# Gated cross attention with a two-expert layer: where statistics, normalisations and gating stand in VectorE's order, and a rebuilt prologue

## The reference

```python
q = (xn @ Wq + bq).reshape(B, T, H, hd)
k = (xfn @ Wk + bk).reshape(B, N, H, hd)
v = (xfn @ Wv + bv).reshape(B, N, H, hd)
w = softmax(einsum('bthd,bnhd->bhtn', q, k) / sqrt(hd))
y = einsum('bhtn,bnhd->bthd', w, v).reshape(B, T, D)
...
logits = xf @ w_router
top_vals, top_idx = top_k(logits, 2)
h = square(relu(einsum('nc,ecd->ned', xf, w1)))
y_all = einsum('ned,edc->nec', h, w2)
out = sum(take_along_axis(y_all, top_idx[:, :, None], axis=1) * softmax(top_vals)[:, :, None], axis=1)
...
x = x + tanh(g_xattn[0]) * xattn(layernorm(x), ctx_768, ...)
x = x + tanh(g_ffn[0]) * ffn(layernorm(x), ...)
```

## Time and profile before

| | |
|---|---|
| time, median of 3 runs | 363.44 us (362.04 to 373.72) |
| the profiled execution | 362.29 us |
| its span | 360.5 us |
| its mean granted TensorE clock | 0.969 |
| instructions | 7799 |

### The profile page before, as it was taken

How to read it: one execution, slowest core, us unless ns; L and a number is a source line. 1 busy time by engine, 2 the same in 40 slices (tenths; PEclk the granted TensorE clock), 3 DMA queues, 4 the chain that set the end, 5 groups by cost and what they waited for, 6 DMA issues and landing times.

```text
span 360.5 us, 7799 instructions
## 1 busy us (share of the span) xinstructions
PE 296.0 (82%) x2823; PEld 242.1 (67%) x2823; DVE 230.1 (64%) x932; ACT 180.8 (50%) x410; POOL 107.7 (30%) x188
## 2 busy tenths in 40 slices
PE   0686988889698979888898979897999899877795
PEld 0444576567576767777677867786788788665684
DVE  5595576567557775777667766778567656534455
ACT  1234454545365546455555646464656455533273
POOL 6381815226113350315131613141132100211000
PEclk9997899999899999999999989999999999989899
DMA  3511401074607453463528270835174520250001
GB/s 81 155 47 31 111 20 49 16 118 90 235 4 111 66 185 126 92 85 108 204 53 125 69 244 24 114 44 194 79 110 60 181 90 3 56 213 0 2 30 30
DMA packets 18918, 32.92 MB, mean 91 GB/s; under 512 B 4921, under 2 KB 12058, under 8 KB 18880
## 3 DMA queue, kind: packets, MB, share of 16 engines
q1 hardware_dynamic: 14814, 24.71, 27.8%
q0 software_dynamic: 3216, 7.66, 8.9%
q10 hardware_dynamic: 850, 0.05, 0.2%
HBM read 21.04 MB, written 2.21 MB: 65 GB/s over the span
## 4 chain that ended last, share of the span: by engine, by line
PE 44%; DVE 24%; DMA 11%; ACT 8%; issue 6%; SPq 2%; DVEq 0%; ACTq 0%
PE y L584 12%; PE c L539 7%; DMA gb<-gates_scratch 5%; DVE u L1082 5%; PE ab L495 5%; ACT hs L796 3%; DMA gates_scratch<-gatesT 3%; DMA qs<-q_lo 2%; PE ab L562 2%; PE ab L437 2%; DVE negm L963 2%; PE ab L445 2%; PE h L470 2%; PE ab L428 2%; SPq L317 1%
## 5 line engine op out<-in xcount | busy, mean ns | idle before, releaser
L963 DVE TENSOR_REDUCE negm<-ab 128x4 f32<-128x308 f32 x128 | 60.3, 474 | 73.3 <-PE ab L495 73.0
L791 ACT ACTIVATE p<-s 77x512 f32<-77x512 f32 x128 | 74.3, 583 | 18.4 <-PE s L516 18.4
L584 PE MATMUL y<-w2s,hs 128*128 128x128 f32 x448 | 66.1, 294 | 17.0 <-ACT hs L796 16.9
L584 PEld LDWEIGHTS y<-w2s,hs 128*128 128x128 f32 x448 | 59.9, 206 | 20.6 <-ACT hs L796 20.3
L516 PEld LDWEIGHTS s<-qs,ks 104*77 104x77 f32 x512 | 53.5, 148 | 12.5 <-issue 4.9
L495 PE MATMUL ab<-ks,qs 96*128 96x312 f32 x128 | 50.5, 397 | 13.6 <-ACT cnT L715 9.6
L516 PE MATMUL s<-qs,ks 104*77 104x128 f32 x512 | 56.8, 234 | 2.7 <-ACT p L791 2.6
L796 ACT ACTIVATE hs<-u 128x512 f32<-128x512 f32 x56 | 35.1, 627 | 34.6 <-DVE u L1082 34.4
L1246 POOL TENSOR_SCALAR rs<-mv 128x1 f32<-128x1 f32 x32 | 7.5, 235 | 122.9 <-DVE mv L1004 122.8
L1082 DVE SCALAR_TENSOR_TENSOR u<-h,gb 128x512 f32<-128x512 f32 x56 | 36.7, 673 | 5.6 <-DMA gb<-gates_scratch 3.7
L495 PEld LDWEIGHTS ab<-ks,qs 96*128 96x128 f32 x128 | 24.8, 194 | 18.9 <-ACT cnT L715 10.7
(11 more groups left out here) (130 smaller groups left out, 512.1 us busy)
## 6 DMA issues: line engine op xcount, KB each, us to landing
gb<-gates_scratch SPq DMA_DIRECT2D x14, 768.0 KB, 6.0
gb<-gates_scratch SPq DMA_DIRECT2D x7, 512.0 KB, 3.7
qs<-q_hi SPq DMA_DIRECT2D x12, 256.0 KB, 5.7
ks<-k_hi SPq DMA_DIRECT2D x60, 39.0 KB
x_res<-in_x_dram POOLq DMA_DIRECT2D x8, 256.0 KB, 8.0
out_dram<-y_out POOLq DMA_DIRECT2D x7, 256.0 KB, 5.5
x_sb<-in_x_dram POOLq DMA_DIRECT2D x6, 256.0 KB, 3.5
qs<-q_lo SPq DMA_DIRECT2D x6, 256.0 KB, 7.6
```

Of the source, the lines that this page charges most:

```text
L584: mm = nc.tensor.matmul(bank_y[:, D * b:D * b + D], hs[:, e % 2, T * b:T * b + T], w2s[:, e, :], start=(e == 0 and b == 0), stop=(e == E - ...
L791: nc.scalar.activation(p32[:, m % LR, :], src, ACT.Exp).then_inc(p_done, 1)
L963: nc.vector.tensor_reduce(negm[:, :, c], bank_ab[bank][:, 0:J * NP].rearrange("t (i n) -> t i n", n=NP)[:, :, 0:N], AX.X, ALU.max, negate= ...
```

## The change

*VectorE, steps 1 to 5:* the statistics of the tile after next stand between the row maxima of slot 0, `normalise_ctx` between those of slot 1, `normalise_x` between those of slot 2 (step 0: statistics in slot 1, normalisation in slot 2). In slots 0 and 1 the residual add and its statistics come after the first gated product; in slot 1 all of `gate` comes ahead of the residual, its last four pieces after the first gated product.

*TensorE and ScalarE:* `transpose_ctx` stands behind `max_turn`, `transpose_x` ahead of the output products of slot 2; `gates_turn` stands ahead of the output products of slot 1, `gate_rows` behind the third exponential. `evacuate_ctxT` stands ahead of slot 2's first square.

*GpSimd:* `norm_rstd` moves from slot 2 to slot 0 (step 0: slot 1), behind `rstd`.

*Prologue:* context of tile 0 first on SP's queue, the input of tile 0 first on ScalarE's; weights counted by four semaphores instead of one; tile 0's keys are projected right after its context transpose; tile 1 is transposed in slot 3 of step -1, its keys and query rows are made in slot 0 of step 0; expert loads go to ScalarE's queue in step -1, `prepare_experts` in four parts to slots 1, 2, 3 of step 0 and 0 of step 1, `low_experts` in two parts; the value tile 0 is cleared by GpSimd, the key tile 1 in eight pieces; fewer `keep_on`. Four uses of the `ab` banks are moved in their order.

```diff
-AB_SHIFT = {name: -shift for shift, name in AB_USES}
...
+AB_MOVED = [(("k", 0), ("ctxT", 0)), (("ctxT", 1), ("mT1", 0)), (("xT", 1), ("s1b2", 0)), (("k", 1), ("s1d2", 0))]
...
+                turned = third if j == (3 if i == -1 else 2) else None
+                made = (1, 1) if (i, j) == (0, 0) else third if j == 3 and i != -1 else None
...
@@ SP
-            load(0, 0)
+            sp.dma_start(ctx_sb[:, 0], ctx_v[0]).then_inc(ctx_first[0], 16)
...
@@ TensorE, step
                     if near[0]:
                         scoresT(*near[0], 2)
                     if j == 1 and nxt:
                         project_values(nxt[0])
-                    if i == -1 and j >= 2:
-                        keep_on(bank_s2[1], 2)
                     if i == 0 or (i == 1 and j < 2):
                         keep_on(bank_h[0], 2)
                     if near[2]:
                         max_turn(*near[2])
-                    if j == 3 and third:
-                        (project_queries if i >= 0 else project_query_rows)(third[0])
+                    if turned:
+                        transpose_ctx(turned[0])
+                    if turned and turned[0] == 0:
+                        project_keys(0)
+                    if made:
+                        (project_queries if made[0] >= 2 else project_query_rows)(made[0])
                     if e[2] is not None:
                         hidden(sf, pf, e[2])
...
-                    if j == 2 and third:
-                        transpose_ctx(third[0])
                     if near[3]:
                         scores(*near[3], 0)
                     if (i, j) == (-1, 3):
-                        keep_on(bank_s2[1], 4)
+                        keep_on(bank_s2[1], 2)
                     if near[1]:
                         scoresT(*near[1], 0)
+                    if j == 1 and spread(i - 1):
+                        gates_turn(i - 1)
                     if e[1] is not None and j != 2:
                         output_of(sf, pf, e[1])
                     if near[3]:
                         scores(*near[3], 1)
-                    if i == 0 or (i == 1 and j < 2):
+                    if (i == 0 and j > 0) or (i == 1 and j < 2):
                         keep_on(bank_h[1], 2 if i else 1)
+                    if turned:
+                        transpose_x(turned[0])
                     if e[1] is not None and j == 2:
                         output_of(sf, pf, e[1])
-                    if j == 2 and third:
-                        transpose_x(third[0])
-                    if j == 1 and spread(i - 1):
-                        gates_turn(i - 1)
@@ ScalarE
+            act.dma_start(x_sb[:, 0], x_v[0]).then_inc(x_first[0], 16)
...
-                    if e[1] is not None:
+                    if turned:
+                        evacuate_ctxT(turned[0])
+                    if turned and turned[0] == 0:
+                        evacuate_k(*turned)
+                    if e[1] is not None and j != 2:
                         squared(sf, e[1])
...
                     if near[0]:
                         exponent(*near[0], 3)
+                    if j == 1 and spread(i - 1):
+                        gate_rows(i - 1)
+                    if e[1] is not None and j == 2:
+                        squared(sf, e[1])
@@ VectorE, step
+                    if third and i >= 0 and j == (1 if i == 0 else 0):
                         prepare = stats(*third)
+                        ahead = prepare
+                    if third and i > 0 and j == 1:
+                        ahead = normalise_ctx(*third)
+                    if third and i > 0 and j == 2:
+                        ahead = normalise_x(*third)
...
                     take(top_scores)
+                    take(ahead)
                     take(top_scores)
+                    take(ahead, 2 if ahead is prepare and j < 2 else 1)
                     take(top_scores)
...
                     if near[-2]:
                         low_x(*near[-2])
-                    take(gating)
-                    take(gating)
-                    take(top_scores)
+                    take(gating, 3)
+                    if j in (2, 3):
+                        take(post)
+                        take(post)
                     if j == 2 and exists(i - 2) and not last(i - 2):
                         finish(i - 2, par)
-                    take(gating)
-                    take(post)
...
+                    if j == 2:
+                        take(post)
+                    if j == 3:
+                        take(prepare)
+                        take(post)
                     if e[1] is not None and not (i >= S and near[-2] and not near[-1]):
                         gated_or_weighed(sf, pf, e[1])
+                    take(gating, 4)
+                    take(post, 3)
+                    take(prepare)
@@ GpSimd, step
                     if (i, j) == (-1, 0):
+                        clear_values(pool, nc.gpsimd, 0)
+                        norm_rstd(1, "ctx")
+                        norm_rstd(1, "x")
+                        for c in range(NC):
+                            for half in range(2):
+                                nc.gpsimd.memset(ks[:, 1, c, 2 * half:2 * half + 2].bitcast(F32),
+                                                 0.0).then_inc(zeroed[1], 1)
...
+                    if (i, j) in ((0, 3), (1, 0)):
+                        low_experts(i)
```

More of the change, by code:

```diff
@@ L41, with ab_sequence @@
 ]
-AB_SHIFT = {name: -shift for shift, name in AB_USES}
-def ab_order(step, tiles):
-    return [name for shift, name in AB_USES
+AB_MOVED = [(("k", 0), ("ctxT", 0)), (("ctxT", 1), ("mT1", 0)), (("xT", 1), ("s1b2", 0)), (("k", 1), ("s1d2", 0))]
+def ab_sequence(tiles):
+    uses = [(name, step + shift) for step in range(-2, tiles + 1) for shift, name in AB_USES
             if 0 <= step + shift < tiles and (name, step + shift) not in (("q", 0), ("q", 1))]
-STATS = ["ctx_stats", "x_stats", "ctx_moments", "x_moments"]
+    for moved, behind in AB_MOVED:
+        uses.remove(moved)
+        uses.insert(uses.index(behind) + 1, moved)
+    return {use: k for k, use in enumerate(uses)}
+STATS = ["ctx_stats", "ctx_moments", "x_stats", "x_moments"]
 NORM = ["ctx_normed", "x_normed"]
@@ L226, in apart @@
             eng.sem_inc(held_apart, 1)
+        ab_turns = ab_sequence(S)
         def ab(s, name):
-            step = s + AB_SHIFT[name]
-            k = sum(len(ab_order(t, S)) for t in range(-2, step)) + ab_order(step, S).index(name)
+            k = ab_turns[name, s]
             return k % 2, k // 2 + 1
@@ L374, in unit_rows @@
                         .then_inc(ones_in[par], 16)
-            unit_rows(0)
             def step(i, par):
-                for j, near, nxt, third, ffn in slots(i, par):
+                for j, near, nxt, third, turned, made, ffn in slots(i, par):
                     if near[2]:
```

208 lines of the change are left out of this document (108 added, 100 removed).

## The result

The changed kernel takes 347.45 us (median of 4 runs, 345.29 to 354.17), the kernel before 366.09 in the same comparison (4 runs, 362.04 to 373.72): a ratio of 0.955, 95% interval 0.945 to 0.965. The profiled execution took 348.87 us against 362.29, so 13.4 of the 29.3 us forecast came. The time lies in the stated range, near its upper end, which stood at 349 for the sake of R1, and outside the likeliest case's own 325 to 342; the size of the change does not agree with the sum behind it.

A forecast was written before the change was run, and what follows sets the result against it. It took the kernel to be bound by TensorE, plus a serial chain per slot from VectorE's order of work, plus a prologue. From 362.3 us, 19.8 for the steps and 9.5 for the prologue gave 333.0; range 324 to 349.

The forecast's parts named there:

- R1: Steady steps: inserted work makes row maxima late, the step stays near 38 us, only the prologue pays; 350 us, chance 0.13.
- the likeliest case: Whole kernel: steady steps and prologue both gain; 333.0 us, own range 325 to 342, chance 0.62.
- Slot 0, 1.2 us: Steady slot 0: statistics between maxima remove the 1.0 us wait for the square, 0.4 of the next 0.6 remains; gain 1.2.
- Slot 2, 2.5 less 0.3: Steady slot 2: context waits of 1.1 and 1.4 us go, gain 2.5, less 0.3 per step for sharing transfers.
- Gating earlier: Slot 1: gating ahead of the residual starts the two transfers behind it some 1.2 us earlier.
- R4: Steady steps: gates come too late for new places on TensorE and ScalarE, prologue costs more; about 358 us, chance 0.08.
- parts 1 and 2: Tile steps: statistics and normalisations between maxima, and gating ahead of the residual; gain 19.8 us, bounds 6 to 25.
- (a): Prologue: split loads and keys projected first bring the first scores 3.0 us earlier, to 19.9; bounds 1 to 4.
- (b): Prologue: first to first transposed scores takes 8 us instead of 19.9, two slots of 3.5 plus filler; gain 8 to 13.
- (c): Slot 0 of step 0: tile 1's keys and query rows moved there cost 4.0 us, plus 1.4 for lower clock.
- R3: Step 0 on: fewer fillers leave TensorE's clock at 0.50 until slot 2 of step 1; 375 us, chance 0.04.
- R2: Prologue: two load queues win nothing, first statistics stay at 6.2 us, prologue gives 4; 338.5 us, chance 0.13.

The follow-up runs named there:

- maximum_first_slot2: Changed kernel with the next batch's first maximum ahead of the second gated product in slot 2; 347.27 us, ratio 0.947 to the kernel before.
- prologue_only: Changed kernel with the old order from step 1 on, keeping the new prologue and step 0; 367.47 us, ratio 1.010 to the kernel before.
- more_fillers: Changed kernel with more filler matmuls in step -1 and ahead of the first transposed scores; 346.57 us, ratio 0.954 to the kernel before.
- all_mended: The last experiment: prologue_mended and maximum_first_slot2 together, plus 3 fillers in slot 1 of step 0; 338.75 us, ratio 0.936 to the kernel before.
- prologue_mended: Changed kernel with no clearing beside the first cast, more fillers in step -1, low query rows ahead of the next maximum; 340.94 us, ratio 0.935.
- slot0_as_before: Changed kernel with VectorE's old order in slot 0 from step 1 on; 359.21 us, ratio 0.990 to the kernel before.

## Why the prediction was right or wrong

**Bottleneck: right.** TensorE's waits behind VectorE's order were what could be won; nearly all of the gain is there (0.958 by itself).

**Slot 0, 1.2 us: measured 0.9** (0.84 to 0.92 in steps 2 to 5). The wait for the square (1.0) went as forecast. The residual's chain, of which I kept 0.4, is late by 0.79. The order is worth more than this difference, though: undone alone, inside the new kernel, slot 0 takes 1.1 to 2.5 us more, and the ratio goes from 0.955 to 0.990, some 12 us. I priced it by its wait, not by the clock that follows: 5.6 us in that run's steps 3 and 4, against 4.4 for the waits of four steps.

**Slot 1, 0: measured -0.35.** The wait for x2 of 0.55 is new: with the gating first, the residual and its normalisation come later in this slot.

**Slot 2, 2.5 less 0.3: measured 1.4 to 2.5, mean 1.9.** Both waits went. Late next was neither the gates nor the square but the bank held by a maximum, 0.85; `maximum_first_slot2` brought 0.6 of it. I had named a maximum that the score matmuls wait for as what would prove me wrong; here the input's transposes wait for one, and it costs a part of the gain.

**Gating earlier, 1.2 us earlier and nothing by itself: too small.** The gates' store went out 6.75 us after the slot's value products (159.27 less 152.52), before it was 8.19 (164.94 less 156.75): 1.4 earlier, as reckoned. But without it the new slot 2 is 2.5 to 3.6 us longer, 1.3 of it the longer wait (2.2 for 0.9), the rest not split; the clock has a part in it (0.91 from 125 to 165 us), and the residual's place may have one. The 356 us are near R4's 358, but not by R4's way: there the gates were too late for their new places on TensorE and ScalarE, here for their use on VectorE, with the places as before. The change as made avoids it. I had no term for what it protects.

**Steps 1, 6 and 7: right.** Slot 2 of step 1 gave 3.7 for 3.0, steps 6 and 7 gave 2.0 for 2.0, and slots 0 and 1 of step 1 nothing, with the forecast wait for tile 2's stack:

```profile
PE ab L503 <- DMA qs<-q_lo: 1.3, 1, 1.3
```

The steady step is 35.6 us, not 34.6, and parts 1 and 2 gave 16.5 of 19.8 us (9.8 + 2.0 + 3.7 + 1.0). This alone would have been a fair forecast.

**The prologue, 9.5 us: this is the step that failed.** It gave minus 3.7 with the slots up to slot 2 of step 1 (without slot 2 of step 0, which is in parts 1 and 2), and nothing when tried alone (1.010). The lower bound of 4 did not follow from its own terms either: 1 + 8 - 8 - 1.4 is -0.4. By its terms:

(a) 3.0 earlier: measured 1.9, within its bounds.

(b) 8 us from first to first transposed scores, 11.9 less than before: measured 12.6, so 7.4 less, under its lower bound of 8. The two slots took 5.3 and 4.05 us where the sum has 3.5 each (20.97, 26.27, 30.32), and 3.2 more passed up to 33.52, with the context transposes of tile 1 and four filler records in 1.91 us, where it has 1. The statement that a piece of clearing "can hold up a cast by no more than itself" is refuted: the cast started at 24.54 and ended at 26.01, as the last of the eight pieces did (25.97), 1.47 us where a piece is 0.57 (4.53 / 8). The rest of the excess is waits and work at 0.50 (1.2 GHz), not split further. The rule of the Trainium skill that I weighed there (SBUF — State Buffer, section "SBUF: two separate sides"), that two-port VectorE work and GpSimd lock a shared port pair for a whole instruction, has the right pair of engines, but my reading of it, that pieces are the cure, does not hold here: 1.47 us of waiting against 0.57 for a piece.

(c) minus 4.0 and 1.4: from first transposed scores to first value products it took 5.9 us before and 15.6 after, 9.6 more instead of 5.4 (6.4 in `prologue_only`), and slot 1 of step 0 adds 2.7 (3.1 there). From 32 to 40 us TensorE is busy for 7.5 of 8 at 0.50: some 4 us are the clock's alone. The row for the clock was in the prediction, and I took 1.4 from it; the point missed is that taking twelve of the twenty filler records out and leaving two slots of waits keeps the clock down longer, over useful work (with 32 more records in `more_fillers` it stayed at 1.00), and that it falls a second time behind the wait for the low query rows (with fillers in that wait, in `all_mended`, it stayed at 1.00 there). In the better executions the clock was back by 36 us, and (c) was too small by 1.0 only. Added up: 9.5 less 1.1 for (a), 4.5 for (b) and 4.2 for (c) is the -0.3 of the table; 2.7 in slot 1 of step 0 and 0.7 behind it make -3.7. R3 had this mechanism and expected it through all of step 0; it ended after 40 us, came again from 50 to 58, in step 0 as my sign of being wrong had it, and cost a few us, not 42. `prologue_mended`, which takes away the clearing beside the cast, the half-empty slots and the low rows' place, brings back some 7 us (0.955 to 0.935): first value products 6.0 before the kernel before, less 1.7 in slot 1, about half of the 9.5. The rest of the 7 lies further on: its steps from slot 2 of step 1 on take 35.4 to 35.6 us without exception, where the changed kernel's profile has two of 36.2 and 36.3.

**R2** was right in this: the second queue wins 0.65 us for the input's statistics and nothing at the first scores. Its sign was not: the first statistics did not stay at 6.2 but start at 4.27, with one queue or two, since they no longer wait for both loads together. The Trainium skill, DMA: Bandwidth & Descriptors, section "Issuing engines are not separate DMA queues", says that only issue time is saved; in the one execution tried that does not cover it, since the input was issued 0.48 us later on the shared queue and landed 1.8 later.

**R1** was the reverse of what happened: the work put between the maxima didn't make them late, except the first one of slot 2, and the steady step did not stay near 38. That its 350 lies close to the measured time is chance, and so is it that the range, stretched to 349 for it, holds the time. Of the chances, 0.91 for faster should be 0.92 by the terms given.

## What to carry to other kernels

An earlier start is worth only what TensorE does with it: where work that kept it busy is taken out from between waits, read the granted clock of the stretch behind them and count with the lower level (here 8 to 12 us at 0.50), and price a wait by what its removal or its return does to the next slots, not by its length. When a bound is read off "the longest wait", ask for what the moved work protects: put the moved work back alone inside the new order, since neither slot 0's order nor slot 1's was worth the same in the old kernel and in the new one. Keep long GpSimd clearing away from VectorE casts by a dependency, not by cutting it in pieces.

## What the runs showed of the hardware that was not expected

- A 16-column cast of VectorE did not get in between GpSimd's memsets: 1.47 us until the end of a row of eight, 2.61 until the end of the next clearing (whose record starts only 0.76 after the cast's), 0.17 with none beside it (0.28 to 0.44 for a later one, with transfers issued by GpSimd beside it). Three row maxima of 0.5 us each ran beside the same memsets undelayed (22.90 to 24.42).
- Executions of one prologue differ by how long the clock stays down: four kernels whose prologue is the changed one to the letter have their first transposed scores at 33.52 to 33.55 us, and their first value products at 45.50, 45.90, 45.92 and 49.07. A single profile of such a stretch is good to some 3 us.
- The length of single waits doesn't tell where the clock falls: slot 3 of step 0 in the last experiment had none over 0.5 us near it, a step of the kernel before kept 1.00 through a wait of 1.44 us (at 173.32), and waits of 0.97 and 0.82 were followed by a fall in step 4 of `slot0_as_before` and by none in step 5.
